# Gathers of a DLRM tower that wait for TensorE's counts by a table

## The reference

```python
e = jnp.stack([tbl_0[ids[:, 0]], ..., tbl_26[ids[:, 26]]], axis=1)
xactions = jnp.einsum('bfd,bgd->bfg', e, e)
z = xactions[:, _TRIL_I, _TRIL_J]
h = jnp.concatenate([z, dense_ctx], axis=1)
h = jnp.maximum(h @ W_top1 + b_top1, 0.0)
h = jnp.maximum(h @ W_top2 + b_top2, 0.0)
y = h @ W_top3
```

## Time and profile before

| what | value |
|---|---|
| runs, median of 3 | 149.44 us (146.7 to 149.49) |
| the profiled execution's own time | 147.56 us |
| its span, first to last instruction | 145.8 us |
| TensorE matmuls busy | 101.9 us, 70% |
| VectorE, ScalarE, GpSimd busy | 72.6, 62.9 and 68.3 us |
| mean granted TensorE clock | 0.871 of full |

### The profile page before, as it was taken

One profiled execution on the slowest core, in us unless ns is written; L12 is line 12 of the kernel. 1 busy time (PEld: TensorE's weight loads), 2 busy tenths in 40 slices (PEclk: granted clock), 3 DMA queues, 4 the chain that ended last, 5 costly groups with the idle time before them and its releaser, 6 DMA issues.

```text
span 145.8 us, 2362 instructions
## 1 busy us (share of the span) xinstructions
PE 101.9 (70%) x920; PEld 84.4 (58%) x920; DVE 72.6 (50%) x156; ACT 62.9 (43%) x109; POOL 68.3 (47%) x67
## 2 busy tenths in 40 slices
PE   0069999989969129996356000079796999889994
PEld 0058888868848027782125000079686888589983
DVE  6697999998999504442300000013737334436321
ACT  4293989996986405430010110032645631335320
POOL 2787888878888777777777775000000000000000
PEclk9999999999999975799655555556999999999999
DMA  5966786665679952221111111000000000000000
GB/s 134 396 215 242 252 264 218 224 197 203 246 232 255 285 164 70 54 58 48 47 48 54 54 54 54 0 0 4 0 4 0 4 0 0 0 4 4 0 0 3
DMA packets 8461, 14.92 MB, mean 102 GB/s; under 512 B 3525, under 2 KB 4037, under 8 KB 8450
## 3 DMA queue, kind: packets, MB, share of 16 engines
q1 hardware_dynamic: 6242, 10.31, 21.4%
q0 software_dynamic: 1920, 3.94, 9.7%
q10 hardware_dynamic: 288, 0.52, 1.2%
HBM read 14.76 MB, written 0.00 MB: 101 GB/s over the span
## 4 chain that ended last, share of the span: by engine, by line
PE 39%; POOL 24%; another core or an unknown queue 12%; issue 8%; DMA 7%; ACT 4%; DVE 4%; DVEq 0%; ACTq 0%
POOL X L208 24%; PE ps_g L266 11%; PE ps_l L301 6%; PE ps_l L230 5%; PE ps_l L228 5%; DMA X<-in_tbl,ids_all 5%; PE ps_l L318 4%; DMA ids_all<-in_ids 2%; PE ps_x L245 2%; PE ps_x L301 2%; ACT ET L577 1%; PE ps_x L318 1%; PE ps_l L331 1%; PE ps_z L285 1%
## 5 line engine op out<-in xcount | busy, mean ns | idle before, releaser
L208 POOL DMA_INDIRECT X<-in_tbl,ids_all x60 | 67.5, 1125 | 20.7 <-issue 18.0
L228 PE MATMUL ps_l<-onehot,high 128*128 128x512 f32 x96 | 42.1, 439 | 13.9 <-ACT high L555 8.4
L452 DVE TENSOR_SCALAR onehot<-ids_row,vocab 128x512 fp32r<-128x512 int32 x84 | 36.4, 489 | 14.1 <-PE ps_l L230 7.3
L230 PE MATMUL ps_l<-onehot,low 128*128 128x512 f32 x96 | 40.6, 423 | 0.0
L266 PE MATMUL ps_g<-ET 128*64 128x54 f32 x512 | 18.8, 240 | 20.5 <-ACT ET L577 16.8
L228 PEld LDWEIGHTS ps_l<-onehot,high 128*128 128x128 f32 x96 | 19.9, 207 | 20.4 <-ACT high L555 8.4
L266 PEld LDWEIGHTS ps_g<-ET 128*64 128x64 f32 x512 | 17.9, 155 | 21.8 <-ACT ET L577 17.1
L230 PEld LDWEIGHTS ps_l<-onehot,low 128*128 128x128 f32 x96 | 20.0, 208 | 3.9
L577 ACT COPY ET<-ps_l 128x512 f32<-128x512 f32 x12 | 13.2, 1098 | 20.1 <-remote 18.1
L465 DVE COPY early<-ps_g 128x216 f32<-128x216 f32 x8 | 3.1, 383 | 33.6 <-PE ps_g L266 33.5
L440 DVE TENSOR_TENSOR low<-early,high 128x1024 fp32r<-128x1024 f32 x12 | 14.7, 1226 | 5.2 <-issue 2.3
(11 more groups left out here) (42 smaller groups left out, 56.0 us busy)
## 6 DMA issues: line engine op xcount, KB each, us to landing
early<-in_tbl_look SPq DMA_DIRECT2D x12, 512.0 KB, 4.9
ids_row<-in_ids_look SPq DMA_DIRECT2D x10, 256.0 KB
X<-in_tbl,ids_all POOLq DMA_INDIRECT x60
ids_row<-in_ids_look ACTq DMA_DIRECT2D x2, 256.0 KB
w<-in_W_top SPq DMA_DIRECT2D x2, 256.0 KB
w<-in_W_top SPq DMA_DIRECT2D x1, 512.0 KB
w<-in_W_top SPq DMA_DIRECT2D x1, 248.0 KB
ids_all<-in_ids SPq DMA_DIRECT2D x1, 54.0 KB, 3.1
```

The source lines that it names most:

```text
L208: pool.indirect_dma_start(out=X[:, t % 2, at, :], out_offset=None, in_=tables[f][:, :], in_offset=bass.IndirectOffsetOnAxis(ap=ids_all[:, ...
L228: pe.matmul(ps_l[f % 2][:, 0:batch], high[:, f % HIGHS, c, :], onehot[:, at % ONEHOTS, :], start=(c == 0), stop=False)
L230: pe.matmul(ps_l[f % 2][:, 0:batch], low[:, f % RING, c, :], onehot[:, at % ONEHOTS, :], start=False, stop=(c == CHUNKS - 1)).then_inc(chu ...
L452: dve.tensor_scalar(onehot[:, at % ONEHOTS, :], ids_row[:, f % ROWS, :], vocab[:, c:c + 1], None, ALU.is_equal).then_inc(onehot_ready, 1)
```

## The change

Two tables of counts are made when the program is built. A gather whose number n is in CHUNKS_BEFORE waits until chunk_done has reached its count: n = 5 to 44, with floor(5 n / 2) - 10, at most 96 (2 at n = 5, 15 at 10, 40 at 20, 65 at 30, 75 at 34, 90 at 40, 95 at 42, 96 at 43 and 44). A gather in QUARTERS_BEFORE, n = 45 to 59, waits until `dots` has reached n - 44, at most 8 (so 1 at n = 45, 7 at 51, and 8 from 52 to 59). Gathers 0 to 4 have no such wait. The waits for `turned` stay.

```diff
 PARTS = [(0, 2), (2, 3), (3, 4)]
 WIDEST = 2 * P
+
+CHUNKS_BEFORE = {n: min(N_LOOK * CHUNKS, 5 * n // 2 - 10) for n in range(5, 45)}
+QUARTERS_BEFORE = {n: min(8, n - 44) for n in range(45, TILES * N_GATHER)}
...
                     if t >= 2:
                         pool.wait_ge(turned, (t - 2) * GROUPS + g + 1)
                     for f in group:
+                        n = t * N_GATHER + at
+                        if n in CHUNKS_BEFORE:
+                            pool.wait_ge(chunk_done, CHUNKS_BEFORE[n])
+                        if n in QUARTERS_BEFORE:
+                            pool.wait_ge(dots, QUARTERS_BEFORE[n])
                         pool.indirect_dma_start(
```

## The result

The changed kernel takes 140.29 us (median of 4 runs, 139.42 to 140.92) against 148.81 for the kernel before beside it: a ratio of 0.951, 95% interval 0.938 to 0.964. It is faster, as forecast, but by 8.5 us and not by 27. The time lies outside the range.

What follows compares the result with a forecast made beforehand. Bound by waits: a dense train of gathers holds up TensorE's counts, paid for from 69 to 95 us. 147.56 - 27.8 gained + 2 of remaining lag = 121.8, forecast as 122.3 us; range 118.5 to 136.

Steps and rivals of the forecast that it cites:

- Part (1): Gathers 5 to 33 in the look-ups: their counts are in before they start, so the waits cost 0.
- Part (4): After the look-ups: products start at 69.8 us, not 95.67 (25.9 gained); tile 0 takes 4.4 us (1.9 gained).
- Parts (2) and (3): Gathers 34 to 44 follow TensorE's chunks until about 71 us; 45 to 59 await product quarters; nothing is late.
- Part (5): Behind product quarter 8: gathers 52 to 59 issue in a row, gather 59 in time; cost 0, bounds 0 to 5.5 us.
- Part (6): Lag of TensorE's counts remaining from chunk 81 on and beside the burst of eight gathers: 2 us, bounds 0 and 25.9.
- Rival C: Among the products: the holding moves to counts that gathers await, 29 to 45 us lost, 149 to 165 total; chance 0.09.
- Rival A: In the look-ups: lag persists from chunk 81, 11 us more, 133 total; chance 0.21 together with a late gather 59.

Runs made afterwards that it cites:

- cut38_c: The changed kernel without gathers 38 to 59: 120.89 us, with the kernel before at 148.82 beside it.
- before_again: The kernel before, unchanged, run again with its trace: 147.55 us.
- quarters_only_b: The changed kernel with the table of chunks emptied and only that of quarters kept: 138.93 us against 146.01 for the kernel before.
- after_again: The changed kernel, unchanged, run again beside the kernel before: 137.03 us against 147.15, ratio 0.932.

## Why the prediction was wrong

The direction was right, and so was most of the working; the size was wrong by one step.

- The reading of the trace holds. A dense train of gathers beside TensorE holds back its counts (cut38_c against the kernel before at one place: 27.9 us by the medians, 25.7 by the lowest times; the forecast had 27.8). That this train does so at some places and times only was not in it.
- Part (1), no cost in gathers 5 to 33: right. From gather 9 on a count of chunks is at times named as what GpSimd waited for, but its idle time stays at 0.30 us. One gather took 3.60 us, where the longest before was 2.02.
- Part (4), look-ups: right. 70.25 for 69.8.
- Part (4), products of tile 0 at 4.4 us: 12.8. A free tile takes 4.5 (cut38_c).
- Parts (2) and (3): gather 44 was to start near 71 us, and next to nothing to stand beside the products of tile 0. It started at 75.60: gather 34 was already 3.0 us later than reckoned, and gather 38 waited for the late count 85. So gathers 40 to 44 stood beside the start of tile 0.
- Part (5), the burst of gathers 52 to 59: priced only by when gather 59 lands. That was right (0.94 us each, the last at 100.11) and beside the point: turn 15 waited for nothing. What the burst costs is tile 2, 10.6 us.
- Part (6) is the step that failed: "I take 2 us for both together, bounds 0 and the whole 25.9". It was 20.5. For the look-ups it held: the lag began again and the loop cut it. For the products I had reasoned that the hold-up needs 14 us of dense gathers to begin, since the counts were prompt before chunk 81, and so that a burst of 10 us is harmless. The burst beside tile 2 held it from 4.2 us on. A difference between the two is that the look-ups give TensorE 2 matmuls in 0.455 us and the products 64 in 2.08, seven times as many; that this is the reason for the faster onset is not shown.
- Rival C had the mechanism, the holding moves into the products. Its price, 29 to 45 us, was read from a kernel whose train never stops; closing the loop bounds each piece to about the train's own length (8.3 us for a train of 8.4, 10.6 for one of 9.7), and 20.5 is less than the 27.8 gained. I gave it 0.09, and the range stopped short of any middle between A and C. Rival A's band, 127 to 144 us, holds the measured time, but by luck: its mechanism was late chunks in the look-ups, and these ended at 69.11.
- That the kernel before itself may take 122 us was in no rival, and the trace of one execution at one place can't show it.

## What to carry to other kernels

Where a count reaches its waiter long after the modelled end of its matmul, or matmuls come singly with idle time by "issue", look at what GpSimd does in that stretch, not at the waiter's line. A wait that paces another engine must keep its work thin all along: releasing eight gathers by one count makes the very train that it was to break. Even spacing beside the tables (1.56 us for 1.25) took the kernel to 130 us, where the tables alone gave 137 to 140, but where nothing is held up spacing cost 1.6% (the same memset, no tables) and 6.4% (the longer memset, with tables). And compare kernels only beside each other at one place and time: the same kernel took 120 and 149 us here.

## What the runs showed of the hardware that was not expected

- Gathers of 0.95 us every 1.25 us stop TensorE almost wholly at some times (ten single matmuls in 17 us) and not at all at others, with the same durations on GpSimd. It is not a chip's property alone: chip 6 was seen both ways.
- What is held is let go a while after the last gather of a train: 1.9 and 2.1 us after its end in the changed kernel, 4.3 us in before_again, 5 us in the kernel before.
- The places and times with the hold-up went with missing records of semaphore updates in every trace seen (70 to 82 of 96, against 96), also in the three kernels whose products were not held up there. Every timed run here lists its granted clock, so each was recorded; that the writing of records takes part in the hold-up, and that it would be absent in an unrecorded run, would fit, but is argued and not shown.
- Before the handfuls begin, 42 to 49 matmuls pass in one run in the changed kernel and quarters_only_b, 35 and 48 in after_again, and 23 in before_again. What sets the number is open.
